# A delta-rule layer on one core: the triangular solve runs on x over its gate, VectorE writes X, the constant products leave the cycles

## The reference

```python
def step(St, inp):
    q_t, k_t, v_t, a_t, b_t = inp
    err = jnp.einsum('bhvk,bhk->bhv', St, k_t) - v_t
    St = a_t[..., None] * St - (b_t[..., None] * err)[..., None] * k_t[:, :, None, :]
    o_t = jnp.einsum('bhvk,bhk->bhv', St, q_t)
    return (St, o_t)
```

## Time and profile before

| | |
|---|---|
| time, median of 3 runs | 2797.2 us (2792.12 to 2802.65) |
| the profiled execution, its time | 2792.46 us |
| its span | 2790.7 us |
| mean granted clock of TensorE | 0.968 |
| TensorE busy | 2578.7 us, 92% |
| VectorE busy | 2042.4 us, 73% |
| GpSimd busy | 1445.2 us, 52% |
| ScalarE busy | 1204.5 us, 43% |
| recurrence | about 954 to 2026 us |
| of it L1197 and L1202 (1792 instructions each) | 328.5 us at 221 ns, 330.8 us at 226 ns |
| of it L787 (448) | 331.6 us at 786 ns |
| of it L879 (128) | 256.2 us of waiting for VectorE in front of it |

### The profile page before, as it was taken

The page is one execution under the profiler, slowest core; times in us unless marked ns, Lnnn a source line. Parts: engine busy times, 40 slices in busy tenths (PEclk is TensorE's granted clock), DMA queues, the critical chain, the costliest instruction groups (busy, mean ns, idle before and its releaser), DMA issues. The chain is left out here.

```text
span 2790.7 us, 50619 instructions
## 1 busy us (share of the span) xinstructions
PE 2578.7 (92%) x17812; PEld 2216.3 (79%) x17922; DVE 2042.4 (73%) x5887; ACT 1204.5 (43%) x2393; POOL 1445.2 (52%) x1216
## 2 busy tenths in 40 slices
PE   8999999999999489999999999999749997899999
PEld 6888888888888378888888888888637776788887
DVE  4776778678769279999999999989768886433333
ACT  4445445544454233333333333323568874433333
POOL 2644553455355489999889898979422220000000
PEclk9999999999999799999999999989859999999999
DMA  5466555655664855555556566555654543100000
GB/s 132 129 177 185 150 146 163 187 143 146 171 179 124 266 201 215 200 198 198 215 227 231 214 230 227 214 197 198 240 202 158 213 188 122 67 12 11 11 11 15
DMA packets 417321, 454.39 MB, mean 163 GB/s; under 512 B 122497, under 2 KB 367233, under 8 KB 393857
## 3 DMA queue, kind: packets, MB, share of 16 engines
q1 hardware_dynamic: 417152, 452.22, 48.6%
HBM read 321.49 MB, written 131.14 MB: 162 GB/s over the span
## 5 line engine op out<-in xcount | busy, mean ns | idle before, releaser
L355 PE MATMUL pa_ps<-pa_x_hi,pa_w_hi 128*128 128x512 f32 x1296 | 507.0, 391 | 9.4 <-ACT pa_y L298 5.2
L355 PE MATMUL pa_ps<-pa_x_lo,pa_w_hi 128*128 128x512 f32 x1296 | 505.1, 390 | 0.0
L355 PE MATMUL pa_ps<-pa_x_hi,pa_w_lo 128*128 128x512 f32 x1296 | 504.9, 390 | 0.0
L438 DVE SCALAR_TENSOR_TENSOR pa_cv<-pa_y,pa_taps,pa_cv 128x2048 f32<-128x2048 f32 x144 | 357.1, 2480 | 17.8
L1197 DVE TENSOR_TENSOR pb_tmp<-pb_gb,pb_ps 128x112 f32<-128x112 f32 (+6 forms) x1792 | 328.5, 221 | 25.5 <-POOL pb_gb L787 11.6
L787 POOL TENSOR_TENSOR pb_gb<-pb_gb,pb_ng 128x448 f32<-128x448 f32 (+6 forms) x448 | 331.6, 786 | 2.9 <-DMA pb_gb<-scratch_pairs 2.9
L1202 DVE TENSOR_TENSOR pb_ps<-pb_ps,pb_tmp 128x112 f32<-128x112 f32 (+6 forms) x1792 | 330.8, 226 | 0.0
L355 PEld LDWEIGHTS pa_ps<-pa_x_hi,pa_w_hi 128*128 128x128 f32 x1296 | 243.6, 188 | 67.1 <-ACT pa_y L298 9.4
L771 POOL TENSOR_TENSOR all_res<-all_res,pb_crow 128x1024 f32<-128x1024 f32 x120 | 281.9, 2367 | 6.1 <-DMA pb_crow<-scratch_crow 6.1
L355 PEld LDWEIGHTS pa_ps<-pa_x_hi,pa_w_lo 128*128 128x128 f32 x1296 | 243.7, 188 | 50.7
L355 PEld LDWEIGHTS pa_ps<-pa_x_lo,pa_w_hi 128*128 128x128 f32 x1296 | 243.6, 188 | 50.0
(11 more groups left out here) (191 smaller groups left out, 5426.9 us busy)
## 6 DMA issues: line engine op xcount, KB each, us to landing
pb_crow<-scratch_crow SPq DMA_DIRECT2D x30, 2048.0 KB, 10.0
pb_gb<-scratch_pairs SPq DMA_DIRECT2D x64, 896.0 KB, 6.6
pa_o_ng<-scratch_beta SPq DMA_DIRECT2D x16, 1024.0 KB, 7.9
scratch_ng<-pa_o_ng SPq DMA_DIRECT2D x16, 1024.0 KB, 4.5
scratch_A<-pa_o_A SPq DMA_DIRECT2D x16, 1024.0 KB, 4.5
scratch_vt<-pa_o_vt SPq DMA_DIRECT2D x16, 1024.0 KB, 4.5
scratch_q<-pa_o_q SPq DMA_DIRECT2D x16, 1024.0 KB, 6.9
scratch_g<-pa_o_g SPq DMA_DIRECT2D x16, 1024.0 KB, 7.8
```

Of the source, the lines that this page charges most:

```text
L355: last = nc.tensor.matmul(out, w[:, mat, k, :], xx[:, k, b * S:(b + 1) * S], start=(k == 0 and n == 0), stop=(k == KT - 1 and n == 2))
L438: nc.vector.scalar_tensor_tensor(out=out, in0=yy[:, :, k:k + S], scalar=tap(k), in1=out, op0=ALU.mult, op1=ALU.add).then_inc(s_tap, 1)
```

## The change

Three edits.

The solve runs on y = x over its gate. Then y of a step is w less the shares of the earlier y, each times the gate of its own, earlier step. So `with_gates` multiplies the row of step t by the gate of step t, a broadcast, instead of by the gates of the later steps; `solve` works in place on w (now `y_of`), and the multiplication by the gates moves from its start to its end. There VectorE writes it straight into X. ScalarE's `copy_x` loses its copy and becomes `transposed_x`; s_xc, which TensorE waits for ahead of the transposes, is now raised by VectorE.

With the multiplication the last reading of `ng` and `ngx` moves: SyncE waits on s_xc (`gated`) for the load of the next gates, ScalarE likewise for its copy to `ngx`.

FILL becomes 0 in every place; the last cycle keeps its 4.

```diff
--- before.py
+++ after.py
@@ -518,8 +518,7 @@
         ps = [m.ps(f"ps{i}") for i in range(8)]
         psT, psD, wx = ps[0:2], ps[2:6], ps[6:8]
 
-        w_of = [t[:, 0:HALF * BL].rearrange("p (h t) -> p h t", t=BL) for t in wx]
-        x_of = [t[:, HALF * BL:2 * HALF * BL].rearrange("p (h t) -> p h t", t=BL) for t in wx]
+        y_of = [t[:, 0:HALF * BL].rearrange("p (h t) -> p h t", t=BL) for t in wx]
 
         s_id = m.sem("id")
         s_mask = m.sem("mask")
@@ -571,7 +570,7 @@
 
         FIRST, MIDDLE, LATE, LAST = range(4)
         SUMS = [0, 0, 0, 0, 0, 0, 0, 4, 8, 11, 16, 21, 25, 29, 34, 39, 44]
-        FILL = [2, 2, 2, 2, 2, 2, 2, 2]
+        FILL = [0, 0, 0, 0, 0, 0, 0, 0]
 
         all_decays = Gm[:, :, :, :, :].rearrange("p g a i t -> p (g a i t)").rearrange("p (c x) -> p c x", c=NCH)
         decay_rows = crow[0:HB, 0:NCH, :]
@@ -584,7 +583,7 @@
         window = lambda w: (slice(16 * w, 16 * w + 16), slice(max(16 * w - BL, 0), 16 * w + BL))
         solved = lambda c, n: 2 * (NBL * c + n + 2)
         turn = lambda c, n, hf: 2 * NBL * c + [[0, 2, 3, 5], [4, 6, 7, 9]][hf][n] - 1
-        scaled = lambda c, n, hf: 27 * turn(c, n, hf) + 1
+        gated = lambda c, n: NBL * c + n + 1
 
         @block.sync
         def _(sp):
@@ -675,8 +674,8 @@
                 load_gb(c + 1, 0)
                 sp.wait_ge(s_m, NBL * (c + 1))
                 sp.wait_ge(s_ngx, c + 1)
-                sp.wait_ge(s_sv, scaled(c, 3, 0))
-                sp.wait_ge(s_sv, scaled(c, 1, 1))
+                sp.wait_ge(s_xc[0], gated(c, 3))
+                sp.wait_ge(s_xc[1], gated(c, 1))
                 load(ng[:, :, :], "ng", c + 1, s_ngl)
                 sp.wait_ge(s_x[1], solved(c, 1))
                 load_gb(c + 1, 1)
@@ -784,7 +783,7 @@
                 for t in range(BL - 1):
                     w = BL - 1 - t
                     pairs = gb[n][:, :, off[t]:off[t] + w]
-                    last = tt(pairs, pairs, ng[:, :, BL * n + t + 1:BL * (n + 1)], ALU.mult)
+                    last = tt(pairs, pairs, ng[:, :, BL * n + t:BL * n + t + 1].broadcast_to([P, HB, w]), ALU.mult)
                 last.then_inc(s_m, 1)
 
             def cycle(c, lower, upper, p, kind):
@@ -873,10 +872,8 @@
                     last = nc.scalar.activation(Gm[:, g:g + 4, a, :, steps], src[:, :, 1 - a, :, part], ACT.Copy)
                 last.then_inc(s_te, by)
 
-            def copy_x(at, past, c, n, hf, between=None):
-
-                act.wait_ge(s_x[hf], solved(c, n))
-                nc.scalar.activation(X[:, HALF * hf:HALF * (hf + 1), BL * n:BL * (n + 1)], x_of[hf], ACT.Copy).then_inc(s_xc[hf], 1)
+            def transposed_x(at, past, c, n, hf, between=None):
+
                 if between:
                     between()
                 for j in range(2):
@@ -908,41 +905,41 @@
                 def last_key():
                     copy_key(at - T_CH, T_FIRST[1][1], 0, 1, 1)
 
-                copy_x(at, past, c, 0, 0, last_key if kind != FIRST else None)
+                transposed_x(at, past, c, 0, 0, last_key if kind != FIRST else None)
                 key(T_LATER, 1, 0, 0)
                 key(T_LATER, 1, 0, 1)
                 absolutes(0)
                 if kind != FIRST:
-                    copy_x(at, past, c - 1, 3, 1, lambda: next_gram(0))
+                    transposed_x(at, past, c - 1, 3, 1, lambda: next_gram(0))
                 else:
                     next_gram(0)
                 next_gram(1)
                 absolutes(1)
-                copy_x(at, past, c, 1, 0, lambda: next_gram(2))
+                transposed_x(at, past, c, 1, 0, lambda: next_gram(2))
                 next_gram(3)
                 absolutes(2)
                 act.wait_ge(s_ngl, 16 * (c + 1))
                 if kind != FIRST:
-                    act.wait_ge(s_sv, scaled(c - 1, 3, 1))
+                    act.wait_ge(s_xc[1], gated(c - 1, 3))
                 nc.scalar.activation(ngx[:, :, :], ng[:, HALF:HB, CH // 2:CH], ACT.Copy).then_inc(s_ngx, 1)
-                copy_x(at, past, c, 2, 0)
+                transposed_x(at, past, c, 2, 0)
                 absolutes(3)
-                copy_x(at, past, c, 0, 1, lambda: key(T_LATER, 1, 1, 0))
+                transposed_x(at, past, c, 0, 1, lambda: key(T_LATER, 1, 1, 0))
                 key(T_LATER, 1, 1, 1)
                 if more:
                     copy_kt(0)
                 absolutes(4)
-                copy_x(at, past, c, 3, 0, (lambda: copy_kt(1)) if more else None)
+                transposed_x(at, past, c, 3, 0, (lambda: copy_kt(1)) if more else None)
                 if more:
                     copy_kt(2)
                     copy_kt(3)
                 absolutes(5)
-                copy_x(at, past, c, 1, 1, (lambda: key(T_FIRST, 0, 0, 0)) if more else None)
+                transposed_x(at, past, c, 1, 1, (lambda: key(T_FIRST, 0, 0, 0)) if more else None)
                 absolutes(6)
                 if more:
                     key(T_FIRST, 0, 0, 1)
                     key(T_FIRST, 0, 1, 0)
-                copy_x(at, past, c, 2, 1)
+                transposed_x(at, past, c, 2, 1)
                 absolutes(7)
 
             for j in range(4):
@@ -954,7 +951,7 @@
                 for j in range(2):
                     copy_key(0, 8 + 2 * hf + j, 0, hf, j)
             over_cycles(act, cycle)
-            copy_x(T_START + T_CH * NCH, {}, NCH - 1, 3, 1)
+            transposed_x(T_START + T_CH * NCH, {}, NCH - 1, 3, 1)
             for k in range(SUMS[-1], 4 * PIECES):
                 absolute(k)
 
@@ -1014,7 +1011,7 @@
                 fill = FILL[2 * n + hf] if past is not T_PAST[LAST] else 4
                 if fill:
                     busy(bank_t(at, t), fill)
-                pe.wait_ge(s_xc[hf], NBL * c + n + 1)
+                pe.wait_ge(s_xc[hf], gated(c, n))
                 if n:
                     pe.wait_ge(s_rs[hf], 3 * c + n)
                 for j in range(2):
@@ -1163,43 +1160,44 @@
                 src = tile(at, D_S[j])[:, :].rearrange("p (h a t) -> p h a t", h=8, a=2)
                 hs = slice(8 * j, 8 * j + 8)
                 cr = rr[p][:, 1, hs, :].unsqueeze(3).broadcast_to([P, 8, NBL, BL])
-                tt(w_of[hf][:, 8 * q:8 * q + 8, :], src[:, :, 0, 0:BL], rr[p][:, 1, hs, 0:1].broadcast_to([P, 8, BL]), ALU.mult)
+                tt(y_of[hf][:, 8 * q:8 * q + 8, :], src[:, :, 0, 0:BL], rr[p][:, 1, hs, 0:1].broadcast_to([P, 8, BL]), ALU.mult)
                 tt(blocks(W[:, hs, :])[:, :, 1:, :], blocks(src[:, :, 0, :])[:, :, 1:, :], cr[:, :, 1:, :], ALU.mult)
                 tt(blocks(O[p][:, hs, :]), blocks(src[:, :, 1, :]), cr, ALU.mult).then_inc(s_de, by)
 
             def first_v(at, c, hf):
                 dve.wait_ge(s_vl, 16 * c + 16)
                 dve.wait_ge(s_de, at + D_S[4 * hf + 3] + 1 + 4)
-                tt(w_of[hf], w_of[hf], vt[:, HALF * hf:HALF * (hf + 1), 0:BL], ALU.subtract).then_inc(s_w, 1)
+                tt(y_of[hf], y_of[hf], vt[:, HALF * hf:HALF * (hf + 1), 0:BL], ALU.subtract).then_inc(s_w, 1)
 
             def solve(c, n, hf, early=0):
 
                 k = turn(c, n, hf) + early
                 if n == 0:
                     dve.wait_ge(s_w, 2 * c + hf + 1)
-                    dve.wait_ge(s_ngl, 16 * (c + 1))
                 else:
                     dve.wait_ge(s_wn[hf], 6 * c + 2 * n)
-                gates = ng[:, HALF * hf:HALF * (hf + 1), BL * n:BL * (n + 1)]
-                if hf and n >= NBL // 2:
-                    dve.wait_ge(s_ngx, c + 1)
-                    gates = ngx[:, :, BL * n - CH // 2:BL * (n + 1) - CH // 2]
-                ws, xs = w_of[hf], x_of[hf]
-                tt(xs, ws, gates, ALU.mult).then_inc(s_sv, 1)
+                ys = y_of[hf]
                 dve.wait_ge(s_m, NBL * c + n + 1)
-                dve.wait_ge(s_sv, 27 * k + 1)
                 quarters = [(q, slice(QUART * q, QUART * (q + 1)), slice(QUART * (2 * hf + q), QUART * (2 * hf + q + 1))) for q in range(2)]
                 for t in range(BL - 1):
                     w = BL - 1 - t
                     for q, qs, hs in quarters:
                         if t:
-                            dve.wait_ge(s_sv, 27 * k + 1 + 4 * (t - 1) + 2 + q + 1)
-                        tt(tmp[:, hs, 0:w], gb[n][:, hs, off[t]:off[t] + w], xs[:, qs, t:t + 1].broadcast_to([P, QUART, w]),
+                            dve.wait_ge(s_sv, 26 * k + 4 * (t - 1) + 2 + q + 1)
+                        tt(tmp[:, hs, 0:w], gb[n][:, hs, off[t]:off[t] + w], ys[:, qs, t:t + 1].broadcast_to([P, QUART, w]),
                            ALU.mult).then_inc(s_sv, 1)
                     for q, qs, hs in quarters:
-                        dve.wait_ge(s_sv, 27 * k + 1 + 4 * t + q + 1)
+                        dve.wait_ge(s_sv, 26 * k + 4 * t + q + 1)
                         done = s_sv if w > 1 else s_x[hf]
-                        tt(xs[:, qs, t + 1:BL], xs[:, qs, t + 1:BL], tmp[:, hs, 0:w], ALU.add).then_inc(done, 1)
```

(13 more changed lines are left out.)

## The result

The changed kernel takes 2777.0 us (median of 21 runs, 2768.25 to 2796.8), the kernel before, beside it on the same chips, 2789.5 us (21 runs, 2781.3 to 2802.65). The ratio is 0.9954, with a 95% interval of 0.9939 to 0.9969: 12.8 us less, between 8.6 and 17. The forecast was 17 us less and 2780 us. It was right in direction and place, and a third larger than what came. That 2777.0 lies 3 us from 2780 is in part luck: the forecast started from 2797.2 us, the median of three runs, and 17 us off 2789.5 would have been 2772.5. By the prediction's own yardstick (0.5%, 14 us) 12.8 us still count as no change, to which it gave 0.30; the interval of the 21 runs leaves out no change.

A forecast was written before the change was run, and what follows sets the result against it. VectorE and TensorE are nearly full; a cycle is VectorE's order plus six waits for TensorE. Middle cycles -17, first and last -4, clock +4: -17 us from 2797.2, so 2780 us; range 2763 to near 2811.

The forecast's parts named there:

- no change: Whole kernel: rival of no gain that counts, within 0.5% (14 us), at about 2793 us; chance 0.30.
- VectorE's own order: VectorE's unbroken work in each solve: moving the gate multiplication saves 0.18 us a cycle, bounds -0.5 and +0.4.
- State 3's wait: VectorE's 1.16 us wait before a state addition, behind X transposes and constant products: shrinks by 0.9 us, bounds 0.3 and 1.16.
- State 1's wait: VectorE's 0.38 us wait before the other half's state addition: becomes about 0.2 us, limited by when a bank is free.
- L1210's and L1166's waits unchanged: Four of VectorE's six waits for TensorE in a cycle, 2.2 us of 3.7 us: untouched by the change.
- A cycle -1.2 us: Each of 14 steady cycles of the recurrence: 0.9 + 0.2 + 0.1 us less, -17 us together, bounds -1 and -28.
- First and last cycle: Where the chain of solve, X, transposes and cross lies open: nine links lose -4 us, bounds 0 and -6.
- The gates' load: Load of `ng`, issued 4 us later: GpSimd idles 0.6 to 2.5 us, cost nothing; rival without cover 2811 us, chance 0.06.
- The broadcast gate: GpSimd's 28 products a cycle with a broadcast factor: might take 1 us less, bounds -1 and +1, hidden.
- The clock, +4 us: TensorE's granted clock: fewer products leave more idling, so half of one more fall, +4 us; bounds -8 and +112.
- A drop of the clock's mean over the recurrence: Sign in the trace after that the forecast is wrong; expected was clock 1.00 but for one or two stretches.
- The rival of a fall in every cycle: Recurrence: transposes don't count as clock activity, so falls come every cycle; every other cycle would give 2824 us; chance 0.12.

The follow-up runs named there:

- e3: The changed kernel, but VectorE multiplies into a PSUM tile and ScalarE copies it to X; 2783.1 us, ratio 0.9965 to the kernel before.
- e1: The changed kernel with the constant products put back, two ahead of each X; 2781.0 us, ratio 0.9962 to the kernel before.
- e2: The kernel before with only the constant products taken out (the last cycle keeps its four); 2788.4 us, ratio 0.9989 to the kernel before.
- e4: The changed kernel with the two key products issued behind the first four state products; 2778.5 us, ratio 0.996 to the kernel before.
- e6: The changed kernel with constant pairs put back at six of a cycle's eight places; 2784.15 us, ratio 0.9984 to the kernel before.
- e10: The changed kernel with four gram staging tiles and all eight constant pairs of a cycle; 2783.1 us, ratio 0.9968 to the kernel before.
- e12: The changed kernel with key products behind state products, four gram staging tiles and four constant pairs; 2773.4 us, ratio 0.993 to the kernel before.
- e5: The changed kernel with four staging tiles for the gram instead of two; 2782.65 us, ratio 0.9965 to the kernel before.
- e7: The changed kernel with the load of the next gates issued behind three more loads; 2871.9 us, ratio 1.0274 to the kernel before.
- e9: The changed kernel with four gram staging tiles, four constant products at three places and two at three others; 2783.7 us, ratio 0.997 to the kernel before.

## Why the prediction was right, and where it was off

**VectorE's own order, -0.18 us a cycle: -0.3 measured.** The exchange came out near its better end: the product follows by 0.46 us, which saves 0.54; the new multiplication takes 0.42 us (predicted 0.41), the next starts 0.34 us behind it, and that costs 0.47. Five profiles agree on the term (the sums at e3); it lies inside the bounds. The prediction's own sum of the cycle has only 0.1 us for it, less than the 0.18 that it had derived and said would count in full or more.

**State 3's wait, 1.16 down by 0.9: 0.71 measured.** This is the step that was mis-sized. The mechanism is as told: e1 takes 0.36 us of it through the earlier X, e2 takes 0.37 through the pairs, which makes 0.73. Counted from VectorE's state addition ahead of it (1245.84 before, 1240.93 after), TensorE reaches the last gram product 0.70 us sooner (predicted 0.75) and the first X transposes 1.15 us sooner (predicted 1.1), and state 3 only 0.71 us sooner. So the gains upstream were right; what was too small was the allowance for the copies, 0.2 us where 0.44 was lost. With the pair gone, TensorE reaches the second half of the transposes before ScalarE has emptied the gram's bank; the prediction had weighed the copies of the transposes' own banks and not the gram copy that shares them.

**State 1's wait, 0.38 to 0.2: 0.18 measured.** The reason given, the bank's release, allowed either edit to bring it; e1 and e2 show that all of it is X's earlier readiness.

**L1210's and L1166's waits unchanged: nearly.** They took back 0.23 us of the cycle (0.36 to 0.52 in one place, 0.57 to 0.64 in another). The prediction took both ends of these stretches as fixed. The runs have the waits in pairs: where state 1's is 0.38 (before, e2, e3), that of L1210 behind it is 0.36, and where it is 0.18 (after, e1, e4, e6, e10, e12), it is 0.52, so 0.16 of the 0.20 won there are lost at once. With these, the cycle adds up: -0.71 - 0.20 + 0.23 - 0.30 = -0.98.

**A cycle -1.2 us: -0.98 measured, and -13.7 instead of -17 over 14.** Then what was not foreseen: the wait behind the staging DMA, 3 us over the recurrence (e5 took it away). ScalarE has it in e1 and e2 alike; TensorE's transposes meet it with the pairs out (before, once in the 14 cycles, for 0.3 us).

**First and last cycle, -4: -4.8 + 0.1.** The sum was right and the division wrong, which is luck: the last cycle alone brought it all. The first gained nothing; in it VectorE waits 21.2 us for GpSimd, and over it the clock was lower.

**The gates' load, nothing: right.** Issued 3.1 us later (predicted 4), waited for by GpSimd 0.57 us (predicted 0.6 to 2.5), by VectorE not at all. e7 measured the price behind the cover. Once the wait on GpSimd is larger than its slack, the cycle loses not the wait's excess alone, as the prediction's and e7's own estimates had it, but this and what the fall of the clock beside it takes.

**The broadcast gate, up to 1 us less on GpSimd: 0.7.** The 14 products shown went from 10.31 to 9.95 us, and all 28 of a cycle from 21.8 to 21.0; at 256 elements there is no gain (731 and 735 ns). Hidden, as said.

**The clock, +4 us: 3 to 7 by the runs' clocks.** Among the 21 runs of the changed kernel the time rises by about 2.3 us for each 0.001 of mean granted clock that is missing, from 2768.25 us at 0.969 to 2796.8 at 0.957; among the runs of the kernel before it is 1.0 to 1.4 us. The means differ by 0.0029 (0.9674 and 0.9645), so 3 to 7 us of the gain are given back. That is an estimate, and a loose one, since the mean clock is no price: a short fall (some 3.4 us at 0.50) made two cycles of before 1.2 us longer and two of after not at all. It is what joins the parts: -13.7 for 14 steady cycles, -4.8 + 0.1 for last and first, +2.2 for the longer cycles without a fall (3.9 us against 1.7), +3 to +7 for the clock, about -9 to -13 in all, against -12.8 (-8.6 to -17) measured. A drop of the clock's mean over the recurrence was among the prediction's signs of being wrong; over whole runs the mean dropped by that 0.0029, too little to turn the result.

The Trainium skill, "TensorE: Matmul & The Clock Gate", Part 4 (PE-mode transpose), says that the full clock does not engage for transposes. The kernel before contradicts it in its `ternary` stage, more plainly than by the row that the prediction shows: with nothing but the transposes of L1667 on TensorE, behind 7 us of idling, the granted clock rose from 0.50 to 1.00.

```profile
2354.00:2358.00 4.00, 0.00 (x0) 0.00 (x0) 2.51 (x2) 0.00 (x0) 0.00 (x0) 0.50 1.00 376
2358.00:2362.00 4.00, 3.97 (x19) 3.98 (x20) 3.78 (x3) 2.33 (x4) 0.00 (x0) 0.50 1.05 391
2362.00:2366.00 4.00, 4.00 (x29) 4.00 (x28) 3.76 (x4) 3.51 (x6) 0.00 (x0) 0.73 1.05 387
2366.00:2370.00 4.00, 3.90 (x31) 3.00 (x29) 3.66 (x3) 4.00 (x8) 0.00 (x0) 1.00 1.05 388
```

The rival of a fall in every cycle did not occur either: in the steady cycles of after the X transposes stand without constant products, among other products, and the granted clock is 1.00 over the whole 63.2 us.

**What stays open** is where the falls come from. The mean clock of the variants does not follow the number of constant products in order. With none it is 0.9646 and 0.9642 (the changed kernel), 0.9658 (e2), 0.9659 (e3), 0.9617 (e5) and 0.9606 (e4); with four pairs 0.9638 (e12), with six 0.9636 and 0.9639; with eight 0.9674 (before), 0.9672 and 0.9656; with the most, e9, 0.9677. The highest have products in all or many places, but e2 and e3 with none are as high as e10 with all. Which place matters, if any, was not separated.

## What to carry to other kernels

When two engines are both nearly full, price a change on one steady cycle: list the few waits of the fuller engine, and for each ask what was the last thing that it waited for, and what is next behind it; here that gave the sign, and three quarters of the forecast size came. Taking an instruction out of a rotation of shared buffers can make the next buffer's release the new last event: here it was an engine that looked idle (ScalarE, busy 30% of the cycle), and behind it a DMA. And where a profiled pair of executions differs by twice what the medians do, look for a rare event in one of them before explaining it.
